# Weighing the values with narrow column ranges in four of five key blocks

## What is computed

```
kh, vh, qh = heads of kv @ Wk.T + bk, kv @ Wv.T + bv, layernorm(x) @ Wq.T + bq
scores = einsum('bqhd,bkhd->bhqk', qh, kh) * scale
attn = softmax(scores)
ctx = einsum('bhqk,bkhd->bqhd', attn, vh)
x = x + tanh(g_xattn) * (ctx @ Wo.T + bo)
x = x + tanh(g_ffn) * moe(layernorm(x))
```

## Time and profile before

| | |
|---|---|
| median of 3 runs | 298.29 us (298.21 to 299.31) |
| the profiled execution | 297.43 us |
| its span, first to last instruction | 295.5 us |
| mean granted TensorE clock | 0.931 |
| TensorE matmuls busy | 256.1 us, 87% of the span, 1806 instructions |
| TensorE weight loads busy | 226.7 us, 77% |
| VectorE, ScalarE, GpSimd busy | 158.0, 127.8, 151.5 us |

### The profile page before, as it was taken

The page is one execution under the profiler, slowest core; times in us unless marked ns, Lnnn a source line. Parts: engine busy times, 40 slices in busy tenths (PEclk is TensorE's granted clock), DMA queues, the critical chain, the costliest instruction groups (busy, mean ns, idle before and its releaser), DMA issues.

```text
span 295.5 us, 5845 instructions
## 1 busy us (share of the span) xinstructions
PE 256.1 (87%) x1806; PEld 226.7 (77%) x1806; DVE 158.0 (53%) x501; ACT 127.8 (43%) x304; POOL 151.5 (51%) x184
## 2 busy tenths in 40 slices
PE   8889889989998999789949759979999999999920
PEld 4676557867886989768738749869999999999920
DVE  3884857436563435656503382923683634347765
ACT  5344512624243670032250442456556565666630
POOL 8757968185588210006781027076347775445540
PEclk9977979999999997799987998989999999999985
DMA  7900068639323000001325002534235337299455
GB/s 225 348 21 1 0 211 286 204 85 326 106 87 93 2 0 1 2 0 71 108 72 155 23 20 97 167 115 152 84 115 171 111 111 249 53 352 340 138 188 196
DMA packets 25838, 37.60 MB, mean 127 GB/s; under 512 B 3497, under 2 KB 22954, under 8 KB 25714
## 3 DMA queue, kind: packets, MB, share of 16 engines
q1 hardware_dynamic: 21074, 20.15, 22.6%
q0 software_dynamic: 3744, 10.24, 9.5%
q10 hardware_dynamic: 992, 6.84, 6.7%
HBM read 24.88 MB, written 18.39 MB: 146 GB/s over the span
## 4 chain that ended last, share of the span: by engine, by line
PE 48%; DVE 18%; POOL 13%; issue 12%; ACT 4%; DMA 3%; ACTq 0%; POOLq 0%; DVEq 0%
PE pV L1289 17%; POOL y_rows L574 8%; PE pM L1289 7%; PE pG L1289 7%; PE pS L1391 6%; POOL slots L566 4%; PE pM L1353 4%; DVE mx L889 3%; DVE st L843 2%; PE pS L1614 1%; PE pS L1642 1%; PE pG L1323 1%; DMA yc<-y_rows 1%; PE pM L1449 1%; DMA x_sb<-in_x 1%
## 5 line engine op out<-in xcount | busy, mean ns | idle before, releaser
L574 POOL DMA_INDIRECT y_rows<-y_sb,dst_i x46 | 45.9, 997 | 33.9 <-ACT y_sb L792 28.5
L1289 PE MATMUL pV<-vb,prob 123*128 123x136 f32 (+1 forms) x320 | 46.4, 300 | 2.4 <-DVE c_sb L903 1.6
L1289 PEld LDWEIGHTS pV<-vb,prob 123*128 123x128 f32 (+1 forms) x320 | 43.7, 208 | 5.0 <-issue 3.4
L1219 DVE TENSOR_TENSOR hT_lo<-pS,hT_hi 128x256 fp32r<-128x256 f32 x46 | 19.5, 424 | 48.2 <-ACT hT_hi L786 47.9
L648 ACT ACTIVATE prob<-pS 123x512 f32<-123x512 f32 (+1 forms) x40 | 22.3, 594 | 29.3 <-PE pS L1391 29.0
L889 DVE TENSOR_REDUCE mx<-pM 128x4 f32<-128x308 f32 x56 | 24.1, 472 | 17.5 <-PE pM L1353 16.6
L566 POOL DMA_INDIRECT slots<-z2a,pos_u x16 | 15.8, 989 | 30.2 <-DVE pos_u L1123 25.8
L779 ACT ACTIVATE h_sb<-pM 128x256 f32<-128x256 f32 x46 | 17.6, 383 | 27.9 <-PE pM L1289 26.6
L566 POOL DMA_INDIRECT slots<-z2b,pos_u x16 | 15.4, 961 | 23.3 <-DVE pos_u L1123 18.5
L1353 PE MATMUL pM<-kb_hi,qT_hi 128*128 128x308 f32 x64 | 21.1, 393 | 7.0 <-DVE mx L889 3.4
L1289 PE MATMUL pM<-win_hi,xT_hi 128*128 x92 | 26.5, 288 | 0.0
(11 more groups left out here) (216 smaller groups left out, 653.2 us busy)
## 6 DMA issues: line engine op xcount, KB each, us to landing
xg<-slots SPq DMA_DIRECT2D x46, 128.5 KB, 3.1
slots<-in_empty ACTq DMA_DIRECT2D x1, 3983.5 KB, 15.6
yc<-y_rows SPq DMA_DIRECT2D x10, 256.0 KB, 5.2
x_sb<-in_x SPq DMA_DIRECT2D x4, 512.0 KB, 7.7
stage<-in_w_in SPq DMA_DIRECT2D x8, 256.0 KB, 2.7
stage<-in_w_out SPq DMA_DIRECT2D x8, 256.0 KB, 2.7
slots<-in_empty ACTq DMA_DIRECT2D x1, 1927.5 KB, 7.7
out<-x_sb SPq DMA_DIRECT2D x6, 256.0 KB, 2.2
```

What stands on the lines that cost most here:

```text
L574: pool.indirect_dma_start(out=y_rows[int(j >= JB)], out_offset=bass.IndirectOffsetOnAxis(ap=dst_i[:, j:j + 1], axis=0), in_=y_sb[:, j % YR ...
L1219: nc.vector.tensor_tensor(hT_lo[:, j % 2, :], pS[:, 1, 0:D], hT_hi[:, j % 2, :].bitcast(F32), ALU.subtract).then_inc(h_lo, 1)
L1289: last = nc.tensor.matmul(out, l, r, start=(n == 0), stop=(n == len(pairs) - 1))
```

## The change

The five matmuls of a token tile are written out in `weigh`. The first key block moves all 136 columns and starts the accumulation; each of the other four reads from `vb`, and adds to pV, only the columns of the heads that its rows belong to: 51, 34, 51 and 34. The semaphore is incremented by the last, as before. No instruction is added, removed or moved on any engine.

```diff
                 off = (i % 2) * 256
-                product(pV[:, i // 2, off:off + HH * VW],
-                        [(prob[0:CLEN[k], (h * CH + k) * BN + i * P:(h * CH + k) * BN + (i + 1) * P],
-                          vb[0:CLEN[k], b // 2, h, k, :]) for k in range(CH)]).then_inc(pv_ps, 1)
+                for k in range(CH):
+                    at = (h * CH + k) * BN + i * P
+                    c0, c1 = (CHEADS[k][0] * VW, CHEADS[k][1] * VW) if k else (0, HH * VW)
+                    last = nc.tensor.matmul(pV[:, i // 2, off + c0:off + c1], prob[0:CLEN[k], at:at + P],
+                                            vb[0:CLEN[k], b // 2, h, k, c0:c1], start=(k == 0), stop=(k == CH - 1))
+                last.then_inc(pv_ps, 1)
```

## The result

The changed kernel takes 307.38 us (305.67 to 308.85, 4 runs) against 298.25 us (295.31 to 299.31, 4 runs) for the kernel before: ratio 1.032, 95% interval 1.022 to 1.042. It is slower by about 9 us. The forecast was 304.0 us, 5.7 us more than before.

A forecast was written before the change was run, and what follows sets the result against it. TensorE's in-order work, mainly weight loads and matmuls into pV, was taken to bound the kernel. 297.43 - 0.6 + 4.1 + 2.2 = 303.1 us, plus 0.86 from profiled run to median, gives 304.0 us; range 297.3 to 308.0.

The forecast's parts named there:

- The price of a pair: Weighing pairs at full clock: 0.112 us for a narrow pair in place of 0.116, as the weight load sets the pace.
- Term 1: Direct gain of 148 narrow pairs before 114.7 us, 0.004 us each: 0.6 us, bounds 0 and 1.0 us.
- Term 2: From 120.8 to 129.1 us: clock stays at half until the scores have run, 4.1 us lost, bounds 0.6 and 6 us.
- The first send: Sign: GpSimd's first row send comes near 137.5 us in place of 134.03.
- The clock came back: Sign: granted clock at half from about 114.7 us without a break until the scores, near 128 to 131 us.
- The mean granted clock: Sign: the mean granted clock in the profile after is below 0.93.
- Term 3: From 159.1 us: last 30 pairs (1.3 us) and transposes of c (0.9) at half clock, 2.2 us lost, bounds 0 and 3.5.
- only two places: Half clock lasts longer only from about 114.7 and 159 us; with both or one, 300 to 306.5 us, chance 0.60.
- The rival with more places: Clock also falls elsewhere, as between 46 and 50 us, where TensorE waits for VectorE: 306 to 310 us, chance 0.18.
- the clock doesn't react: Rival: narrow pairs leave the clock as it was, only the pairs' gain stays: 297.5 us, chance 0.16.
- moved columns set the price of a pair: Rival: a narrow pair takes 0.036 us, kernel faster at 284.6 us; chance 0.06 together with a lucky clock.

The follow-up runs named there:

- cols_68: Key blocks 1 to 4 move 68 columns, against 136 in the kernel before and 34 or 51 in the changed one: 305.54 us against 298.20 before, ratio 1.030.
- cols_102: Key blocks 1 to 4 move 102 columns, against 136 in the kernel before: ratio 1.018 in the first comparison, 1.003 in the second, on another chip.
- narrow_b2: Narrow columns only in token block 2 (8 calls), 136 columns elsewhere, against the kernel before: 302.64 us against 295.94, ratio 1.035.
- changed_again: The changed kernel without further edit, compared a second time with the kernel before: 305.96 us (7 runs) against 298.20, ratio 1.033.

## Why the prediction was right

**The price of a pair**, 0.112 us in place of 0.116: right. A call of ten took 1.21 us in place of 1.32; less the last matmul, 0.207 us, that is (1.21 - 0.207) / 9 = 0.111 us. At half clock the 20 pairs from 128.20 to 132.50 us took 4.30 us; 4.32 was worked out.

**Term 1**, a gain of 0.6 us before 114.7: right in kind and size (0.7 us between 55 and 113 us), but covered in this pair of executions by 1.1 us of the setup and 1.3 us of the fall at 52.2.

**Term 2**, 4.1 us: the steps took 0.59, -0.07, 0.43, 1.9 and 0.9 us more. From 122.50 to 134.50 are 12.0 us, from 120.78 to 129.09 were 8.3: 3.7 us. The first send came at 139.64 us, 5.6 later (137.5 was named, 3.5 later); the difference is what had gathered before. The clock came back only at 140.9 us, where I had named 128 to 131: that the first group of scores would bring it back was wrong (8.4 us of mostly wide work, with gaps). That cost nothing in the end, since GpSimd led in between: TensorE is 5.4 us late at 134.50 us and again at 164.58 us. The mean granted clock was 0.884, under the 0.93 named.

**Term 3**, 2.2 us: 1.1 for the 30 pairs and 0.9 for the transposes' own length (1.97 against 1.09 us). Its size was nearly right, its end was not: the transposes of 128 columns, which were to bring the clock back, did not. The half clock lasted until 178.5 us and caught the first expert tiles too. From the transposes of c to the last matmul 1.4 us were lost, their own 0.9 among them, so that term 3 came to 2.5 us.

**What fell short.** The forecast of 5.7 us is 3.4 below the 9.1 measured by the medians, and 2.7 below the 8.4 us by which the span of the profiled execution grew. Those 2.7 us are 1.1 us in the setup and 0.5 us behind the last matmul, in which no weighing runs, 1.3 us from the fall at 52.2 us, and 0.3 us more in term 3, less the 0.4 us that term 2 and 0.1 us that term 1 differ the other way. So the step of the forecast that fell short is its choice that the clock stays full before 114.7 us and only two places are at half clock. The rival with more places, given 0.18, is what the profiles show: 52.2 us in one, 85.8 us in the other, where the forty narrow pairs alone took 3.8 us more. Whether the fall at 52.2 us is the change's own is not settled (falls near there came in seven of nine profiles with fewer columns, in none of four without). The forecast's own range for two places, 300 to 306.5 us, does not hold the 307.38 us; the stated range, up to 308.0, does, by 0.6 us. That is less than single executions scatter, and so partly luck. With the second comparison (7.8 us) the excess is 2.1 us.

**The rivals.** That the clock doesn't react is refuted by cols_68 against cols_102 and by narrow_b2. The Trainium skill (TensorE: Matmul & The Clock Gate, section "What's actually happening") has the clock follow how busy the engine was. If busy is read as the share of time with a matmul in the profile, the runs disagree: forty narrow pairs were issued without a gap in changed_again, in a stretch with 13.70 of 13.70 us busy, and the clock stayed at half. That moved columns set the price of a pair is refuted by 128-column and 8-column router pairs taking almost the same time, and by the narrow pairs at 0.111 us.

## What to carry to other kernels

Before columns are cut from a matmul, look whether its weight load already sets the pace: then almost nothing is gained (0.005 us of 0.116 a pair here). Here the cut cost some 3%, because at half clock the narrow pairs did not bring the clock back. Look for the places where the clock is already at half, and ask what brings it back. Compare several executions, since the falls lie elsewhere in each.

## What was not expected

The same code gives falls at different places. The kernel before ran from 291.08 to 299.30 us in one group of 11 runs on one chip, and the changed one from 302.40 to 313.38 us in 7. A difference of under 1% cannot be read off single profiles of this kernel. Moving useless columns, where the weight load sets the pace, cost at most 0.1 us for 16 pairs and kept the clock at full behind the router. It did not shorten this kernel measurably: at one of the two places VectorE's chain took over, and the gain at the other is within the scatter.
